# Attention's last unit: half of its low parts on VectorE, loads ahead behind the last maxima, and no wait for a store at the border

## The reference: a transformer block on an image

```
x = x + L0(group_norm(x))          # attention along the width
    q, k, v = conv_1x7(x @ W + b)  # one 256x256 matrix for each channel, then a convolution over channels and width
    q, k = rope(q), rope(k)
    a = softmax(q k^T / sqrt(256)) # 8 heads of width 32, 512 x 512 scores, for each entry and channel
    o = conv_1x1((a v) @ Wo + bo)  # mixes the channels
x = x + L1(group_norm(x))          # a 3x3 convolution sampled on a sphere
```

## Time and profile before

| | |
|---|---|
| median of 3 runs | 1157.39 us (1154.14 to 1162.59) |
| the profiled execution's own time | 1156.79 us |
| its span, first to last instruction | 1154.9 us |
| mean granted clock of PE | 0.974 |
| busy share of PE, DVE, ACT, POOL | 91%, 72%, 59%, 65% |
| `attend` | about 371 to 895 us of the span |

### The profile page before, as it was taken

One profiled execution on the slowest core, in us unless ns is written; L12 is line 12 of the kernel. 1 busy time (PEld: TensorE's weight loads), 2 busy tenths in 40 slices (PEclk: granted clock), 3 DMA queues, 4 the chain that ended last, 5 costly groups with the idle time before them and its releaser, 6 DMA issues. The chain is left out here.

```text
span 1154.9 us, 25535 instructions
## 1 busy us (share of the span) xinstructions
PE 1051.2 (91%) x10288; PEld 564.1 (49%) x10288; DVE 827.7 (72%) x1210; ACT 682.9 (59%) x1146; POOL 745.9 (65%) x768
## 2 busy tenths in 40 slices
PE   0899999999997999999999999999976888799997
PEld 0677777777773233333333333333323344354553
DVE  5888776666669988999888888888831865544343
ACT  3857677777652666666666666666664322446345
POOL 1144455545553799999999999899975129919900
PEclk9999999999997899999999999999988899999999
DMA  9934434341654939174544628191050999766661
GB/s 304 324 99 139 117 90 142 101 133 40 159 140 125 151 78 159 44 109 85 95 77 77 112 68 127 38 155 45 14 156 37 292 321 282 222 222 162 203 201 48
DMA packets 137589, 158.62 MB, mean 137 GB/s; under 512 B 17808, under 2 KB 85664, under 8 KB 137340
## 3 DMA queue, kind: packets, MB, share of 16 engines
q1 hardware_dynamic: 114368, 122.15, 44.0%
q10 hardware_dynamic: 14560, 25.66, 6.1%
q0 software_dynamic: 8544, 9.18, 3.1%
HBM read 106.11 MB, written 52.89 MB: 138 GB/s over the span
## 5 line engine op out<-in xcount | busy, mean ns | idle before, releaser
L1349 POOL TENSOR_TENSOR a_pl<-a_prob 128x512 bf16<-128x512 f32 x416 | 455.7, 1125 | 52.6 <-ACT a_prob L1306 50.8
L1306 ACT ACTIVATE a_prob<-a_col 128x512 f32<-128x512 f32 x512 | 279.7, 598 | 152.5 <-PE a_col L1217 151.9
L1265 DVE TENSOR_REDUCE a_negmax<-a_row 128x1 f32<-128x512 f32 x384 | 244.5, 679 | 40.8 <-PE a_row L1197 40.6
L548 PE MATMUL f_acc<-f_wh,f_xhl 128*32 128x384 bf16 x2560 | 163.5, 327 | 1.0 <-DVE f_yl L666 1.0
L666 DVE TENSOR_TENSOR f_yl<-f_acc,f_yh 128x768 bf16<-128x768 f32 x80 | 75.3, 956 | 75.8 <-ACT f_yh L780 75.8
L1276 DVE TENSOR_TENSOR a_pl<-a_prob 128x512 bf16<-128x512 f32 x96 | 108.4, 1130 | 24.8 <-ACT a_prob L1306 24.7
L903 POOL TENSOR_TENSOR f_straight<-f_straight,f_turned 128x832 f32<-128x832 f32 x40 | 85.5, 2137 | 59.4 <-DVE f_turned L692 59.4
L1622 PE MATMUL b_acc_s<-b_xh,b_mat_h 128*104 128x512 bf16 x256 | 99.5, 389 | 14.3 <-DVE b_xl L1706 13.2
L1197 PE MATMUL a_row<-a_k,a_q 96*128 96x512 bf16 x256 | 98.1, 383 | 10.9 <-DVE a_negmax L1265 8.9
L548 PE MATMUL f_acc<-f_wl,f_xhl 128*32 128x384 bf16 x1280 | 107.8, 326 | 0.0
L1217 PE MATMUL a_col<-a_q,a_k 98*128 98x512 bf16 x256 | 95.8, 387 | 7.6 <-DMA a_q<-a_maxrows 5.5
(11 more groups left out here) (166 smaller groups left out, 1989.6 us busy)
## 6 DMA issues: line engine op xcount, KB each, us to landing
X<-b_x ACTq DMA_DIRECT2D x16, 526.0 KB, 8.7
a_v<-V SPq DMA_DIRECT2D x16, 512.0 KB, 5.3
Z<-a_z ACTq DMA_DIRECT2D x32, 256.0 KB, 2.2
b_res<-X SPq DMA_DIRECT2D x38, 208.0 KB
out<-b_y ACTq DMA_DIRECT2D x38, 208.0 KB
V<-f_vout SPq DMA_DIRECT2D x64, 104.0 KB
b_raw<-X SPq DMA_DIRECT2D x24, 258.0 KB, 8.1
q<-in_x SPq DMA_DIRECT2D x6, 1024.0 KB, 6.5
```

What stands on the lines that cost most here:

```text
L548: last = nc.tensor.matmul(acc[half][c * KW:(c + 1) * KW, part, 0:PART], xx[g % 2][:, (half * QUAD + c) * FH + f, at], ww[half * QUAD + c][ ...
L1265: nc.vector.reduce_max(negmax[n % PAIR][:, 0, t:t + 1], row[ROW_PLACE[step][0]][:], AX.X, negate=True).then_inc(max_done, 1)
L1306: nc.scalar.activation(prob[sets_done % RING][:, t % QUAD, :], col[step % COLS][:], ACT.Exp).then_inc(exp_done, 1)
L1349: nc.gpsimd.tensor_tensor(pl[p][:, r, :], prob[p][:, r, :], ph[p][:, r, :], ALU.subtract).then_inc(lo_pool, 1)
```

## The change

Three edits. (1) In unit 15 DVE computes the low parts of all 16 odd steps, where it computed six, and in unit 14 eight, where it computed six (`LOWS_AT_END`); POOL's shares fall from 26 to 16 and from 26 to 24. (2) Before its loads ahead, SP also waits until the turned maxima of unit 15 have landed. (3) The wait of ACT for the stores of Z at the end of `attend` is gone. The two tiles z and their semaphores are allocated outside `attend`, under the names `z` and `z_stored`, and SP waits for the stores in `blend` before it loads the first pair of the second entry (pair 8), the first that reads what the last unit stored.

```diff
--- before.py
+++ after.py
@@ -931,7 +931,7 @@
                     clear_pad(g)
 
 
-def attend(nc, T, QK, V, Z, mixing, spaces, q0, k0, qk0_in, negmax0, ahead_in):
+def attend(nc, T, QK, V, Z, mixing, spaces, q0, k0, qk0_in, negmax0, ahead_in, z, z_stored):
 
 
 
@@ -954,6 +954,7 @@
         ROWS = 3
         COLS = 3
         LOWS_ON_DVE = (1, 5, 9, 23, 26, 30)
+        LOWS_AT_END = {UNITS - 2: (1, 5, 9, 23, 25, 27, 29, 31), UNITS - 1: range(1, STEPS, 2)}
         ident = sb("a_ident", [P, P])
         ident16 = sb("a_ident16", [P, P], BF16)
         ones = sb("a_ones", [P, DH], BF16)
@@ -973,7 +974,6 @@
         logs = [sb(f"a_logs{s}", [P, W]) for s in range(2)]
         inverse = [sb(f"a_inverse{s}", [P, W]) for s in range(2)]
         oT = [sb(f"a_oT{s}", [P, FH, W]) for s in range(2)]
-        z = [sb(f"a_z{s}", [P, W]) for s in range(FH)]
         row = [ps(f"a_row{s}", [P, W]) for s in range(ROWS)]
         col = [ps(f"a_col{s}", [P, W]) for s in range(COLS)]
         mix = ps("a_mix", [P, W])
@@ -1004,7 +1004,6 @@
         divided = sem("a_divided")
         out_full = sem("a_out_full")
         out_kept = sem("a_out_kept")
-        z_stored = [sem(f"a_z_stored{s}") for s in range(FH)]
 
         def entry(n):
 
@@ -1018,13 +1017,13 @@
 
             return t // (QUAD * QT) * QUAD + t % QUAD, t % (QUAD * QT) // QUAD
 
-        def low_on_pool(t):
-
-            return t not in LOWS_ON_DVE
+        def lows_on_dve(n):
+
+            return LOWS_AT_END.get(n, LOWS_ON_DVE)
 
         def dve_lows(n, g):
 
-            return len(LOWS_ON_DVE) * n + sum(t < QUAD * (g + 1) for t in LOWS_ON_DVE)
+            return sum(len(lows_on_dve(m)) for m in range(n)) + sum(t < QUAD * (g + 1) for t in lows_on_dve(n))
 
         def pool_lows(n, g):
 
@@ -1057,7 +1056,7 @@
             return [(STEPS * n + t, lambda n=n, t=t: emit(n, t)) for n in range(UNITS) for t in range(STEPS) if STEPS * n + t >= EARLY]
 
         def lows(first, emit, on_pool):
-            return [(STEPS * n + first + t, lambda n=n, t=t: emit(n, t)) for n in range(UNITS) for t in range(STEPS) if low_on_pool(t) == on_pool]
+            return [(STEPS * n + first + t, lambda n=n, t=t: emit(n, t)) for n in range(UNITS) for t in range(STEPS) if (t not in lows_on_dve(n)) == on_pool]
 
         def sets(first, emit):
             return [(STEPS * n + first + QUAD * g, lambda n=n, g=g: emit(n, g)) for n in range(UNITS) for g in range(SETS)]
@@ -1168,6 +1167,7 @@
             sp.wait_ge(mixing_in, 16 * (KR + 3 + FULL_TAPS + len(LAST_AT) + 1))
 
             half = UNITS - CHANNELS
+            sp.wait_ge(max_in[(UNITS - 1) % PAIR], 16 * ((UNITS - 1) // PAIR + 1))
             sp.wait_ge(col_full, STEPS * half)
             for j in range(FH):
                 sp.wait_ge(z_stored[j], 16 * half)
@@ -1329,8 +1329,6 @@
 
             pipeline(quads(KEEP, log_weight) + units(TURN + 1, keep_max) + units(TURN + 2, load_max) + steps(EXP, exp) + quads(KEEP, invert)
                      + tails(TAIL + QT, keep_out) + tails(TAIL + QT + 1, store_z))
-            for j in range(FH):
-                act.wait_ge(z_stored[j], 16 * UNITS)
 
         @block.gpsimd
         def _(pool):
@@ -1352,7 +1350,7 @@
 
 
 
-def blend(nc, T, Z, X1, XP, out, mixing, spaces, ahead_in):
+def blend(nc, T, Z, X1, XP, out, mixing, spaces, ahead_in, z_stored):
 
 
 
@@ -1503,6 +1501,9 @@
         def _(sp):
             def load_pair(g):
                 b, n, s = g // PAIRS, g % PAIRS, (g - AHEAD) % U
+                if g == PAIRS:
+                    for j in range(FH):
+                        sp.wait_ge(z_stored[j], 16 * B * C)
                 if g >= AHEAD + U:
                     sp.wait_ge(acc_full, 2 * (g - U) + 2)
                 load_mixed(sp, Z, z[s][:], b, n, z_in[s])
@@ -1871,8 +1872,10 @@
         w_taps = sb("w_taps", [P, 2, C, C])
         mixing = wmix, bmix, group, slot, table, w_taps
         ahead_in = [sem(f"ahead_in{g}") for g in range(AHEAD)]
-        attend(nc, T, QK, V, Z, mixing, spaces, q0, k0, qk0_in, negmax0, ahead_in)
-        blend(nc, T, Z, X1, XP, out, mixing, spaces, ahead_in)
+        z = [sb(f"z{s}", [P, W]) for s in range(FH)]
+        z_stored = [sem(f"z_stored{s}") for s in range(FH)]
+        attend(nc, T, QK, V, Z, mixing, spaces, q0, k0, qk0_in, negmax0, ahead_in, z, z_stored)
+        blend(nc, T, Z, X1, XP, out, mixing, spaces, ahead_in, z_stored)
 
 
 
```

## The result

| | before | changed |
|---|---|---|
| median | 1159.36 us (4 runs, 1154.14 to 1162.59) | 1145.81 us (4 runs, 1145.0 to 1146.29) |
| profiled execution, its own time | 1156.79 | 1146.29 |
| span | 1154.9 | 1144.5 |
| mean granted clock of PE | 0.974 | 0.983 |

A forecast was written before the change was run, and what follows sets the result against it. Waits in unit 15, before the last set and at the border were taken to bound the third stage's start; 5.3 + 2.2 + 2.0 + 0.9 + 1.9 = 12.3 us off 1156.8 gave 1144.5 us, range 1141 to 1149.5.

The forecast's parts named there:

- Edit 2, the wait itself: Before unit 15's first column scores: PE's 5.50 us wait for the turned maxima almost vanishes, 5.3 us gained.
- Rival 2: At unit 15's maxima: the wait stays because something other than the loads held it; 1152.0 us, chance 0.06.
- The clock behind the stall: In the three sets after unit 15's maxima: PE no longer runs at the lower clock level, 2.2 us gained.
- Edit 1, the end of unit 15: Before the last set: PE's wait for POOL's low parts shrinks, 2.0 us gained, with 0.6 and 2.3 as ends.
- the signs I gave for being wrong: Maxima wait above 1 us; DVE low parts at 1.5 us, PE waiting for DVE; third stage longer than 260 us.
- rival 1: In the last three sets: ports serialise, a pair of low parts costs 1.73 us; 1.4 us lost, 1145.9, chance 0.15.
- Rival 5: From 845.3 on: low parts block each other outright, 3.05 us a pair; slower, 1167.2 us, chance 0.04.
- The tail: From last set to last store's issue: clock may stay up; 0.9 us gained, the middle between 0 and 2.0.
- Edit 3: At the border before the third stage: most of 2.23 us after the last store's issue goes, 1.9 us gained.
- Rival 4: At the border: the meeting of the engines takes the 1.9 us itself; 1146.4 us, chance 0.08.
- The third stage runs as before: Third stage, from 895.37 to the end: starts 12.3 us earlier, its length unchanged since its data has landed.
- rival 3: Third stage gives some back: a 20.39 us transfer among loads and stores lands 4 us later; 1148.5, chance 0.12.

The follow-up runs named there:

- the second job: The changed kernel once more, unedited, against the kernel before: ratio 0.9888 (0.9863 to 0.9912), median 1145.76 us.

## Why the prediction was right, point by point

- **Edit 2, the wait itself (5.3): right**, 5.20. The transfer had been held by the loads ahead: PE gets going 2.54 or 2.55 us behind its issue in all eight profiles where they wait. Rival 2 falls. The size leans on the one profile from which it was read; against the other three without edits 1 and 2 the gain is 4.2 to 4.9. The loads ahead, later by some 4 us, cost nothing that shows.
- **The clock behind the stall (2.2): right with all edits in**, 2.18, and 1.5 to 2.0 against the other three profiles. With edit 2 alone the clock stays up as well, but the time is lost again before the last two sets, because POOL had used the stall to catch up. The prediction booked 7.5 us to edit 2 and 2.0 to edit 1; the runs with one edit each, against the first profile of the kernel before, say 5.3 and 1.3, and 2 us that come only with both. That the terms could be added was an assumption of the sum; it did no harm because both edits were in.
- **Edit 1, the end of unit 15 (2.0): too large**, 1.12. The step that failed is that the low part of step 31 "can start at 878.59", as soon as its exponential is done. In the changed kernel the last exponential ended at 873.98, and DVE began this low part at 875.28, 1.30 us later: behind the division it still had three others to make, of 1.41, 1.52 and 1.52 us. The low part itself took 0.68 us, since POOL had finished, where I had 1.13. So the last set began 2.13 us behind the last exponential; 3.23 it was before, and 1.2 was forecast. The price of a pair, 1.45 us, was right; wrong was what I made of it, a delay of "about 3 x 0.27 = 0.8 us at most, of which the wait for exponential 31 hides most". Low parts of DVE at 1.5 us in the median, and PE waiting for DVE, were among the signs I gave for being wrong, and both came. To take one low part out of DVE's queue did not help, because the last one then ran beside POOL, in 1.52 us; to leave POOL idle at the end did, by 0.6 and 0.7 us. The rule of the Trainium skill in "SBUF — State Buffer", section "SBUF: two separate sides" is borne out in kind again: DVE's low part takes 0.69 us with POOL idle, and twice that beside it. A lock for the whole of each operation would make a pair 1.73 us, and 1.45 was measured, so rival 1 had the place right and the price too high: the last low part ended 1.98 us behind the last exponential, where rival 1 had up to 2.5 and I had 1.13. Rival 5, at 3.05, is far away.
- **The tail (0.9): a middle between two cases, and the first pair of profiles has the lower**, 0.10. One pair does not settle it. The piece depends on when the clock falls: it took 11.3 to 13.9 us in the five profiles without edit 1 (mean 12.6), and 9.7 to 12.3 in the six with it and without the nine matmuls (mean 11.3). What makes the clock fall in one execution and not in another is open. A term of this kind belongs in the range and not in the sum.
- **Edit 3 (1.9): right**, 1.76. In all eight profiles that have the edit the third stage begins 0.46 or 0.47 us behind the last store's issue; I had 0.3. Rival 4 falls.
- **"The third stage runs as before": right as a mean only.** It lasts 253.1 to 259.5 us over thirteen profiles of eleven kernels, in which its own code is the same but for edit 3's wait on SP, so one profile can't tell rival 3 from nothing. In the 35 runs of the kernel before in one job the times lie between 1153.07 and 1163.48 us. The range of 1141 to 1149.5 held the median, and needed that width.
- **The total.** The five terms gave 10.36 us and not 12.3; edit 1 and the tail were each too large by 0.8 to 0.9. The whole is 10.5 us between the two profiled executions, and 11.8 by the ratio (0.0102 of 1157). The median is 1.3 us above the forecast. The gain of 1.0% lies on the line of 1% that the prediction drew through its cases; more runs of both, 0.9888 in the second job, leave it there.

## What to carry to other kernels

Before a wait is taken away, ask who was catching up in it: here 2 of 7.4 us came only when POOL's load was cut as well. A small transfer for which an engine is about to wait is worth issuing before large loads, or these can wait for its landing (here 7.75 us from issue to use became 2.55); look for the same pattern wherever loads are issued in bulk. Where two engines slow each other, ask how late the queue of the one that makes the last piece will be when that piece is wanted, and not only what the piece costs. Where one execution's pieces vary by more than the effect, compare pieces between fixed instructions, and not spans.

## What was not expected

- A DVE low part of two SBUF inputs took 0.68 us with POOL idle and 1.52 us beside POOL's own (1.47 in the median over the last unit), in the same kernel. In unit 15 DVE alone (32 of them) was 0.6 us ahead of DVE and POOL with 16 each.
- The two products behind the last set took 1.99 us each at granted clock 1.00 in both profiles with nine unread matmuls in front of them, and in one of eleven without; in the others one or both took up to 3.78.
- The kernel before has the stall of edit 2 a second time, at unit 1, in some executions: from unit 1's maxima to unit 2's 32.0 us in one profile and 34.7 in the other.
- Left open: what moves the third stage between 253 and 260 us. Its chain holds transfers of some 20 us in a crowd, but no run here varied them.
